# Attention blocks of six matmul rounds against a round of maxima and blocks of five

## The chip, the cores and the metric

The kernel runs on one core of one Trainium2 chip. The metric is the device time of one execution in microseconds (us). A core has five engines that run side by side and wait for one another by semaphores: TensorE (PE in the profile; its weight loads are listed apart as PEld), VectorE (DVE), ScalarE (ACT), GpSimd (POOL) and SyncE (SP), which here only issues DMAs. TensorE writes into PSUM, which has eight banks of 512 fp32 columns; ScalarE and VectorE read them.

## The reference

The program is one network of three layers on x of 8 images x 128 channels x 1024 positions. The first, where the change lies, is attention with 8 heads of 16 channels over the 1024 tokens of an image:

```python
qkv = (tokens @ w_proj + b_proj).reshape(B, N, NUM_HEADS, 3 * HEAD_DIM)
q, k, v = jnp.split(qkv, 3, axis=-1)
attn = jnp.einsum('bihd,bjhd->bijh', q, k) * SCALE
attn = jax.nn.softmax(attn, axis=2)
res = jnp.einsum('bijh,bjhd->bihd', attn, v).reshape(B, N, NUM_HEADS * HEAD_DIM)
out = res @ w_out + b_out + tokens
```

A spiking attention and a mixture of experts with 8 experts follow on its result; the change does not touch them.

## The kernel before

**Steps and blocks.** The attention goes through 16 steps (8 images, two groups of four heads each), and each step through 16 blocks, so 256 blocks. A block holds four score tiles, one for each head: 128 keys x 512 queries in one PSUM bank. A score tile is the sum of two matmuls on different halves of TensorE's rows: its A half contracts rows 0 to 49, its B half rows 64 to 111 (three bf16 parts stand for one fp32 number, and the two extra rows of the A half carry the subtracted maximum). An A matmul and a B matmul that stand side by side run at the same time; such a pair is called a round. ScalarE then takes exp of each tile (L644) into the tile `probs`, and four fp32 matmuls that run beside one another multiply it with v (L556, called pv). The pv of block t-1 is issued behind the rounds of block t.

**Maxima.** Softmax needs the row maximum of scores before exp. So the same scores are also computed the other way round, 128 queries x 512 keys, as two half tiles for each of 512 "maxima": one on A rows (L507, from `twin_q` and `twin_k`), one on B rows (L505, from the stacks). VectorE reduces each half tile to its maximum (L730) in the order in which they were filled; 1024 reductions in all. They run ahead of the scores that need them: the first 22 maxima are made before the first block, and a job called "solo" is one round that holds both halves of one maximum. A normal block makes two maxima, four half tiles; the last 13 blocks have none left to make.

**Banks.** Score tiles and the results of most side jobs share a ring of four PSUM banks (`ring`), taken in turn in the order in which they are begun; a bank can be begun again when ScalarE has read it. Half tiles of maxima and the transposes of the attention's result ("oturn") share a second ring of three banks (`slot`), which VectorE reads. `acc`, where pv sums up, is the eighth bank. TensorE works strictly in order: an instruction whose bank is not free holds up everything behind it.

**Order.** `job_order` gives each job a number, sorts by it, and all engines run through this one list. Between the pv of block t-1 and block t+1 there may be side jobs: "proj" and "v" (projections of the next image), "mturn" (a small matmul, L582, that turns 16 finished maxima into rows; result in the ring, taken by ScalarE at L677), "oturn" (L607; result in the slots, taken by VectorE at L769 and L771), "back", "out" and "bias" (results in the ring, taken by ScalarE), and, on VectorE alone, the statistics of finished tokens (L781, L787). Of the 243 blocks with maxima to make, 92 have nothing on TensorE between the pv before them and themselves, and do not follow an oturn with statistics; these are called plain blocks below. 29 have an mturn there, 29 an oturn, and 7 come straight behind an oturn block and statistics. The other 86 have a proj, v, back, out or bias there. The last 13 blocks, without maxima, are 8 plain ones, one with an mturn, two with an oturn, one with a back and one with an out.

**Rounds.** `ROUNDS` says what stands in a block's rounds. In a pair the first number is what goes on the A rows, the second on the B rows; 0 to 3 are the block's score tiles, 4 and 5 its first and second maximum. The first time that a number appears the tile is begun, the second time a score tile is finished. ScalarE's exps stand in the order in which tiles are finished, the ring banks in the order in which they are begun.

Of the kernel before, what the change touches and what calls it, by code (L numbers as in the profile page):

```python
# [45 lines left out]
BLOCKS = 2 * KT  # L46
# [9 lines left out]

ROUNDS = ((0, 4), (1, 5), (2, 0), (3, 1), (4, 2), (5, 3))


def side_jobs(s):

    b, g = s // G, s % G
    jobs = [(10 if g == 0 else 26 - BLOCKS, "oturn", (s, 0))]
    if s:
        jobs.append((2, "oturn", (s - 1, 1)))
    for n in (0, 1):
        q = 2 * s + 1 + n
        if q < 2 * UNITS:  # L70
            jobs.append((5 if q == 1 else 4 + 8 * n, "mturn", (q,)))
    if g == 0:
        if b + 1 < B:
            jobs += [(at, "proj", (b + 1, n)) for n, at in enumerate((0, 1, 3, 5))]
        if b:
            jobs += [(6, "back", (b - 1, 1)), (8, "out", (b - 1, 2)), (9, "out", (b - 1, 3))]
        else:
            jobs.append((7, "bias", ()))
    else:
        if b + 1 < B:  # L80
            jobs += [(6, "v", (b + 1, 0)), (8, "v", (b + 1, 1))]
        jobs += [(13, "back", (b, 0)), (14, "out", (b, 0)), (15, "out", (b, 1))]
    return jobs


def job_order():

    placed = []

    def put(at, kind, args):  # L90
        placed.append((at, len(placed), kind, args))

    m = AHEAD_FIRST
    for t in range(STEPS * BLOCKS):
        maxima = min(2, 2 * UNITS * QB - m)
        put(10 * t, "block", (t // BLOCKS, t % BLOCKS, m, maxima))
        put(10 * t + 12, "pv", (t // BLOCKS, t % BLOCKS))
        m += maxima
        if t % 2 and m < 2 * t + 2 + AHEAD_MAX and maxima:
            for n in range(2):  # L100
                put(10 * t + 7, "solo", (m + n,))
            m += 2
    for s in range(STEPS):
        for at, kind, args in side_jobs(s):
            t = s * BLOCKS + at
            put(10 * t + 4, kind, args)
            if kind == "out":
                put(10 * t + 23, "stats", args)
                put(10 * t + 42, "aggr", args)
    t = 10 * STEPS * BLOCKS + 20  # L110
    for n, (kind, args) in enumerate([("oturn", (STEPS - 1, 1)), ("back", (B - 1, 1)),
                                      ("out", (B - 1, 2)), ("out", (B - 1, 3)), ("stats", (B - 1, 2)),
                                      ("stats", (B - 1, 3)), ("aggr", (B - 1, 2)), ("aggr", (B - 1, 3))]):
        put(t + n + 30, kind, args)
    placed.sort(key=lambda j: j[:2])
    first = [("proj", (0, n)) for n in range(4)] + [("v", (0, n)) for n in range(2)]
    first += [("solo", (n,)) for n in range(QB + 1)] + [("mturn", (0,))]
    first += [("solo", (n,)) for n in range(QB + 1, AHEAD_FIRST)]
    return first + [j[2:] for j in placed]


def halves(job):
# [8 lines left out]
    met, out = set(), []  # L131
    for pair in ROUNDS:
        for tile, n in enumerate(pair):
# [17 lines left out]


ORDER = job_order()
USES = [use for job in ORDER for use in begun_by(job)]
S_USE = {use: n for n, use in enumerate(u for u in USES if u[0] in S_KINDS)}
# [1533 lines left out]
```

## Time and profile before

| what | us |
| --- | --- |
| median of 3 runs | 1243.26 (1242.04 to 1245.73) |
| the profiled execution's own time | 1240.29 |
| its span (first to last instruction) | 1238.5 |
| TensorE busy | 1094.5 |
| VectorE busy | 877.3 |
| ScalarE busy | 806.8 |
| GpSimd busy | 307.6 |

The profile is one execution. A page gives sums by engine and by group of instructions; the timeline gives instructions in order of time. In the timeline neighbouring instructions of one line are merged into one row with a count, whose duration reaches from the first start to the last end; a bracket names the idle time of the engine before the row and what ended it. The attention takes the span from about 60 to 806 us; the granted clock of TensorE is at its full level there.

### The profile page before, as it was taken

Reading aid. Unit: us, or ns where it says so; the run is one execution under the profiler, and the core shown is the slowest. Engines: PE = TensorE matmul, PEld = TensorE weight load, DVE = VectorE, ACT = ScalarE, POOL = GpSimd, SP = SyncE. Lnnn points to the kernel's source line nnn. Section 1 sums busy time; section 2 is a strip of 40 time slices with the busy share of each in tenths; the row PEclk is TensorE's granted clock in tenths of the full one; section 3 lists DMA queues with packets and bytes.
Section 4 is the critical chain, followed back from the end, with each engine's and each line's share of the span. In section 5 each row is a group of like instructions: output and inputs, shape, how many; then the busy total and the mean of one; then the engine's idle time right before and its main releaser. Section 6 shows DMA issues by size and latency. Waiting matters only on the chain. (4 is left out here: it accounts for less than half of the span.)

```text
span 1238.5 us, 23604 instructions
## 1 busy us (share of the span) xinstructions
PE 1094.5 (88%) x8048; PEld 537.0 (43%) x8048; DVE 877.3 (71%) x1988; ACT 806.8 (65%) x1732; POOL 307.6 (25%) x375
## 2 busy tenths in 40 slices
PE   5999999999999999999999999988877653898974
PEld 2123333333333333333333333335645443888873
DVE  4899879879879878988988988516565633444435
ACT  2177777777777777777877877865756541455542
POOL 4131041041041032022113100104354333444440
PEclk7699999999999999999999999998889855999996
DMA  5528028018108206405504600006000001222219
GB/s 128 106 70 158 1 60 150 27 34 171 25 2 179 48 1 143 85 2 105 123 2 92 120 2 2 18 1 169 19 26 27 24 28 54 62 62 61 62 46 272
DMA packets 73355, 85.52 MB, mean 69 GB/s; under 512 B 15656, under 2 KB 57256, under 8 KB 71704
## 3 DMA queue, kind: packets, MB, share of 16 engines
q1 hardware_dynamic: 64248, 72.65, 27.1%
q0 software_dynamic: 4320, 8.89, 2.0%
q10 hardware_dynamic: 4672, 2.49, 0.9%
q8 instruction: 68, 1.11, 0.4%
q14 instruction: 47, 0.39, 0.1%
HBM read 57.08 MB, written 26.65 MB: 68 GB/s over the span
## 5 line engine op out<-in xcount | busy, mean ns | idle before, releaser
L730 DVE TENSOR_REDUCE neg_half<-slot 128x1 f32<-128x512 f32 x1024 | 633.8, 682 | 101.5 <-PE slot L505 84.1
L644 ACT ACTIVATE probs<-ring 128x512 f32<-128x512 f32 x1024 | 528.7, 603 | 135.1 <-PE ring L514 132.6
L514 PE MATMUL ring<-stack_q,stack_k 50*128 50x512 bf16 (+1 forms) x2048 | 419.2, 382 | 2.0
L556 PE MATMUL acc<-probs,v_sb 128*32 128x512 f32 x2048 | 272.7, 605 | 0.1
L514 PEld LDWEIGHTS ring<-stack_q,stack_k 50*128 50x128 bf16 (+1 forms) x2048 | 151.9, 93 | 257.1 <-issue 109.3
L507 PE MATMUL slot<-twin_k,twin_q 48*128 48x512 bf16 x512 | 182.7, 391 | 20.4 <-DMA twin_q<-parts_dram 12.3
L505 PE MATMUL slot<-stack_k,stack_q 48*128 48x512 bf16 x512 | 162.1, 392 | 2.8 <-DVE neg_half L730 2.8
L1502 ACT ACTIVATE hid_t<-ps_h,b_of 128x128 f32<-128x128 f32 x284 | 80.9, 368 | 79.5 <-PE ps_h L1466 74.6
L424 POOL CAST m_parts<-neg_max 128x16 bf16<-128x16 f32 x32 | 6.3, 196 | 380.2 <-DVE neg_max L736 380.2
L1446 POOL DMA_INDIRECT rows_tok<-y,x_in x71 | 71.1, 1001 | 99.2 <-DVE y L1526 99.2
L1466 PE MATMUL ps_h<-xt,w_of 128*128 128x128 f32 x568 | 78.2, 282 | 17.6 <-DVE w_of L1516 16.6
L507 PEld LDWEIGHTS slot<-twin_k,twin_q 48*128 48x128 bf16 x512 | 47.5, 93 | 95.1 <-DVE neg_half L730 73.0
L993 POOL DMA_INDIRECT rows_in<-z_all,pos x64 | 62.7, 980 | 100.8 <-DVE pos L1325 76.5
L1466 PEld LDWEIGHTS ps_h<-xt,w_of 128*128 128x128 f32 x568 | 70.6, 196 | 21.0 <-DVE w_of L1516 19.4
L1475 PE MATMUL ps_y<-w_sb,hid_t 128*128 x568 | 75.8, 277 | 0.4 <-ACT hid_t L1502 0.4
L1475 PEld LDWEIGHTS ps_y<-w_sb,hid_t 128*128 128x128 f32 x568 | 69.8, 194 | 0.6 <-issue 0.6
L556 PEld LDWEIGHTS acc<-probs,v_sb 128*32 128x32 f32 x2048 | 40.3, 108 | 58.0 <-issue 52.0
L1164 ACT ACTIVATE mask<-bank 128x512 bf16<-128x512 f32 (+1 forms) x80 | 33.5, 465 | 45.4 <-PE bank L1075 43.3
L440 POOL CAST parts<-full 128x512 bf16<-128x512 f32 x28 | 17.1, 610 | 149.6 <-ACT full L687 149.6
L1526 DVE TENSOR_TENSOR y<-ps_y,b_sb 128x128 f32<-128x128 f32 x71 | 20.5, 289 | 40.1 <-PE ps_y L1475 38.6
L471 POOL TENSOR_SCALAR xr<-xr,b_sum 128x1024 f32<-128x1024 f32 x8 | 22.8, 2844 | 94.2 <-DMA xr<-in_x 94.2
L1515 DVE COPY b_of<-b_sb 128x4 f32 x71 | 11.9, 167 | 39.9 <-issue 22.2
(161 smaller groups left out, 1146.3 us busy)
## 6 DMA issues: line engine op xcount, KB each, us to landing
parts_dram<-parts SPq DMA_DIRECT2D x30, 384.0 KB, 5.7
stack_k<-parts_dram SPq DMA_DIRECT2D x16, 384.0 KB, 6.2
stack_q<-parts_dram SPq DMA_DIRECT2D x32, 192.0 KB, 7.5
x_in<-rows_in SPq DMA_DIRECT2D x71, 64.5 KB, 1.9
xp<-in_x SPq DMA_DIRECT2D x8, 512.0 KB, 4.6
stack_k<-parts_dram SPq DMA_DIRECT2D x16, 256.0 KB, 3.8
xr<-in_x SPq DMA_DIRECT2D x8, 512.0 KB, 4.5
out<-out_t SPq DMA_DIRECT2D x16, 256.0 KB, 2.1
```

Source lines behind the costliest of these rows:

```text
L505: return pe.matmul(out[:, :], stack_q[u % STACK_BUFS][rows, qhalf, h, cols], stack_k[u % STACK_BUFS][rows, h, HALF:N], start=True, stop=True)
L507: return pe.matmul(out[:, :], twin_q[u % TWIN_BUFS][:, qhalf, h, cols], twin_k[u % TWIN_BUFS][:, h, :], start=True, stop=True)
L514: return pe.matmul(out[:, :], stack_k[s % STACK_BUFS][rows, h, kt * P:(kt + 1) * P], stack_q[s % STACK_BUFS][rows, half, h, :], start=star ...
L556: mm = pe.matmul(acc[32 * h:32 * h + 32, :], v_sb[s // G % 2][:, kt, s % G * HG + h, :], probs[:, j % PROBS, h, :], start=(kt == 0), stop= ...
L644: act.activation(probs[:, j % PROBS, h, :], ring[n % S_BANKS][:, :], ACT.Exp).then_inc(s_empty[n % S_BANKS], 1)
L730: dve.tensor_reduce(neg_half[q % 2][:, half, k:k + 1], slot[n % M_BANKS][:, :], AX.X, ALU.max, negate=True).then_inc(m_empty[n % M_BANKS], 1)
L993: pool.indirect_dma_start(rows_in, bass.IndirectOffsetOnAxis(ap=pos[:, t:t + 1], axis=0), z_all[:, t, :], None).then_inc(s_sent, 16)
L1164: act.activation(mask[b % 2][:, m, lo:hi], bank_of(job)[:, 0:hi - lo], ACT.Sign).then_inc(s_taken["act"], 1)
L1446: pool.indirect_dma_start(rows_tok, bass.IndirectOffsetOnAxis(ap=x_in[:, s % X_RING, C:C + 1].bitcast(U32), axis=0), y[:, s % Y_RING, :], ...
L1466: mm = pe.matmul(ps_h[s % 2][:, k * P:(k + 1) * P], w1_of[:, s % 2, k * P:(k + 1) * P], xt[:, s % 2, :], start=True, stop=True)
L1475: mm = pe.matmul(ps_y[s % 2][:, 0:C], hid_t[:, s % 2, k * P:(k + 1) * P], w2_flat[:, bass.ds(start + k * C, C)], start=(k == 0), stop=(k = ...
L1502: last = act.activation(hid_t[:, s % 2, k * P:(k + 1) * P], ps_h[s % 2][:, k * P:(k + 1) * P], ACT.Gelu, bias=b1_of[:, s % 2, k:k + 1])
```

## The change

A block has five rounds in place of six and only one of its two maxima in them. The other maximum becomes a solo round, which the list places directly in front of the block, behind the pv and the side jobs that precede it. The rounds are numbered r1 to r6 before; after it the solo round is called r0 and the block's rounds r1 to r5. The four half tiles of maxima are called x0 to x3 and the score tiles s0 to s3. Tile s2 is now begun on the B rows and finished on the A rows. The last 13 blocks, which make no maxima, have no solo round.

```diff
--- before.py
+++ after.py
@@ -56,7 +56,7 @@
 
 
 
-ROUNDS = ((0, 4), (1, 5), (2, 0), (3, 1), (4, 2), (5, 3))
+ROUNDS = ((0, 4), (1, 2), (3, 0), (2, 1), (4, 3))
 
 
 def side_jobs(s):
@@ -93,7 +93,9 @@
     m = AHEAD_FIRST
     for t in range(STEPS * BLOCKS):
         maxima = min(2, 2 * UNITS * QB - m)
-        put(10 * t, "block", (t // BLOCKS, t % BLOCKS, m, maxima))
+        if maxima:
+            put(10 * t - 1, "solo", (m,))
+        put(10 * t, "block", (t // BLOCKS, t % BLOCKS, m + 1, maxima // 2))
         put(10 * t + 12, "pv", (t // BLOCKS, t % BLOCKS))
         m += maxima
         if t % 2 and m < 2 * t + 2 + AHEAD_MAX and maxima:
```

**TensorE, a plain block (step 7), before.** L514 with a `ring` bank is a half of a score tile, L505 and L507 with a `slot` bank a half tile of a maximum; two rows make a round.

```order
L514 MATMUL ring2<-stack_q2,stack_k2 128x512
L505 MATMUL slot2<-stack_k0,stack_q0 128x512
L514 MATMUL ring3<-stack_q2,stack_k2 128x512
L505 MATMUL slot0<-stack_k0,stack_q0 128x512
L514 MATMUL ring0<-stack_q2,stack_k2 128x512
L514 MATMUL ring2<-stack_q2,stack_k2 128x512
L514 MATMUL ring1<-stack_q2,stack_k2 128x512
L514 MATMUL ring3<-stack_q2,stack_k2 128x512
L507 MATMUL slot1<-twin_k0,twin_q0 128x512
L514 MATMUL ring0<-stack_q2,stack_k2 128x512
L507 MATMUL slot2<-twin_k0,twin_q0 128x512
L514 MATMUL ring1<-stack_q2,stack_k2 128x512
```

**The same place after.** All line numbers of the changed kernel are higher by two here.

```order
L509 MATMUL slot2<-twin_k0,twin_q0 128x512
L507 MATMUL slot0<-stack_k0,stack_q0 128x512
L516 MATMUL ring2<-stack_q2,stack_k2 128x512
L507 MATMUL slot1<-stack_k0,stack_q0 128x512
L516 MATMUL ring3<-stack_q2,stack_k2 128x512
L516 MATMUL ring0<-stack_q2,stack_k2 128x512
L516 MATMUL ring1<-stack_q2,stack_k2 128x512
L516 MATMUL ring2<-stack_q2,stack_k2 128x512
L516 MATMUL ring0<-stack_q2,stack_k2 128x512
L516 MATMUL ring3<-stack_q2,stack_k2 128x512
L509 MATMUL slot2<-twin_k0,twin_q0 128x512
L516 MATMUL ring1<-stack_q2,stack_k2 128x512
```

The half tiles of maxima stood in rounds 1, 2, 5 and 6; now two stand in r0, one in r1 and one in r5. The score tiles are begun in rounds 1, 2, 2 and 3 of the block in place of 1, 2, 3 and 4, counted from the first round behind the pv in rounds 2, 3, 3 and 4.

**TensorE around an oturn (step 7), before.** The transpose takes slot0.

```order
L556 MATMUL acc<-probs,v_sb0 32x512 x4
L607 MATMUL slot0<-ident,o_sb 128x128 x4
L514 MATMUL ring2<-stack_q2,stack_k2 128x512
L505 MATMUL slot1<-stack_k0,stack_q0 128x512
L514 MATMUL ring3<-stack_q2,stack_k2 128x512
L505 MATMUL slot2<-stack_k0,stack_q0 128x512
L514 MATMUL ring0<-stack_q2,stack_k2 128x512
L514 MATMUL ring2<-stack_q2,stack_k2 128x512
L514 MATMUL ring1<-stack_q2,stack_k2 128x512
L514 MATMUL ring3<-stack_q2,stack_k2 128x512
L507 MATMUL slot0<-twin_k0,twin_q0 128x512
```

**The same place after.**

```order
L558 MATMUL acc<-probs,v_sb0 32x512 x4
L609 MATMUL slot0<-ident,o_sb 128x128 x4
L509 MATMUL slot1<-twin_k0,twin_q0 128x512
L507 MATMUL slot2<-stack_k0,stack_q0 128x512
L516 MATMUL ring2<-stack_q2,stack_k2 128x512
L507 MATMUL slot0<-stack_k0,stack_q0 128x512
```

Slot0, which the oturn has filled, was asked for again in the block's fifth round (the last row before, x2); it is now asked for in r1, the sixth row after, also by x2.

**ScalarE, the exps of a block and the m_rows of an mturn behind them, before and after.** The number behind `ring` is the bank.

```order
L644 ACTIVATE probs<-ring0 128x512
L644 ACTIVATE probs<-ring1 128x512
L644 ACTIVATE probs<-ring2 128x512
L644 ACTIVATE probs<-ring3 128x512
L677 ACTIVATE m_rows1<-ring0 32x128
L644 ACTIVATE probs<-ring1 128x512
```

```order
L646 ACTIVATE probs<-ring0 128x512
L646 ACTIVATE probs<-ring2 128x512
L646 ACTIVATE probs<-ring1 128x512
L646 ACTIVATE probs<-ring3 128x512
L679 ACTIVATE m_rows1<-ring0 32x128
L646 ACTIVATE probs<-ring1 128x512
```

The second and the third exp have changed places; nothing else has moved on ScalarE, and on VectorE, GpSimd and SyncE nothing at all.

## Rows read from the trace of the kernel before

**Rows 1.** The page: span, then each engine's busy time, share and instructions.
```profile
span 1238.5 us, 23604 instructions
...
PE 1094.5 (88%) x8048; PEld 537.0 (43%) x8048; DVE 877.3 (71%) x1988; ACT 806.8 (65%) x1732; POOL 307.6 (25%) x375
```

**Rows 2.** The page's costliest groups: out<-in, count | busy us, mean ns | idle before, releaser.
```profile
L730 DVE TENSOR_REDUCE neg_half<-slot 128x1 f32<-128x512 f32 x1024 | 633.8, 682 | 101.5 <-PE slot L505 84.1
```

**Rows 3.** Waits of TensorE's weight loads, 100 to 780 us: total us, times, longest.
```profile
PEld slot L507 <- DVE neg_half L730: 58.7, 224, 0.5
```

**Rows 4.** Timeline, 316 to 327 us: start, duration, engine, line, tiles, count [idle before].
```profile
318.44 5.06 DVE L730 TENSOR_REDUCE neg_half<-slot 128x1 f32<-128x512 f32 x8 [1.13 <-PE slot L505]
...
320.56 0.09 PEld L514 LDWEIGHTS ring<-stack_q,stack_k 50*128 50x128 bf16 x1 [0.84 <-issue]
...
321.00 0.61 PE L514 MATMUL ring<-stack_q,stack_k 50*128 50x512 bf16 x4
...
321.44 0.38 PE L507 MATMUL slot<-twin_k,twin_q 48*128 48x512 bf16 x1
...
321.51 2.06 ACT L644 ACTIVATE probs<-ring 128x512 f32<-128x512 f32 x4 [0.51 <-PE ring L514]
...
321.76 0.09 PEld L507 LDWEIGHTS slot<-twin_k,twin_q 48*128 48x128 bf16 x1 [0.23 <-DVE neg_half L730]
...
322.09 0.16 PEld L556 LDWEIGHTS acc<-probs,v_sb 128*32 128x32 f32 x8 [0.23 <-issue]
...
323.08 0.97 PEld L598 LDWEIGHTS ring<-w_all,xp 128*128 128x128 f32 x8 [0.84 <-issue]
```

**Rows 5.** Timeline of VectorE, 300 to 400 us: four reductions that are ready in time.
```profile
346.09 2.48 DVE L730 TENSOR_REDUCE neg_half<-slot 128x1 f32<-128x512 f32 x4 [1.13 <-PE slot L505]
```

**Rows 6.** Timeline, 329 to 332 us: a block with an output transpose (L607) before it.
```profile
329.27 0.42 PEld L607 LDWEIGHTS slot<-ident,o_sb 128*128 128x128 f32 x4 [0.84 <-issue]
...
329.86 0.09 PEld L514 LDWEIGHTS ring<-stack_q,stack_k 50*128 50x128 bf16 x1 [0.17 <-issue]
...
330.26 0.42 DVE L771 TENSOR_TENSOR o_t<-slot,inv 128x256 f32<-128x256 f32 x1
...
330.61 7.55 DVE L730 TENSOR_REDUCE neg_half<-slot 128x1 f32<-128x512 f32 x12
...
330.74 0.09 PEld L507 LDWEIGHTS slot<-twin_k,twin_q 48*128 48x128 bf16 x1
...
331.66 0.16 PEld L556 LDWEIGHTS acc<-probs,v_sb 128*32 128x32 f32 x8 [0.23 <-ACT probs L644]
```

**Rows 7.** Timeline, 333 to 337 us: a block with a turn of the maxima (L582) before it.
```profile
333.61 2.06 ACT L644 ACTIVATE probs<-ring 128x512 f32<-128x512 f32 x4 [0.73 <-PE ring L514]
...
334.18 0.16 PEld L556 LDWEIGHTS acc<-probs,v_sb 128*32 128x32 f32 x8 [0.23 <-issue]
...
335.21 0.09 PEld L514 LDWEIGHTS ring<-stack_q,stack_k 50*128 50x128 bf16 x1 [0.48 <-ACT probs L644]
...
335.72 0.24 PEld L514 LDWEIGHTS ring<-stack_q,stack_k 50*128 50x128 bf16 x4 [0.40 <-ACT probs L644]
...
336.74 0.16 PEld L556 LDWEIGHTS acc<-probs,v_sb 128*32 128x32 f32 x8 [0.23 <-issue]
```

**Rows 8.** Timeline of TensorE, 382 to 388 us: the block behind an output transpose with statistics.
```profile
382.52 0.39 PE L505 MATMUL slot<-stack_k,stack_q 48*128 48x512 bf16 x1
...
384.66 1.07 PE L556 MATMUL acc<-probs,v_sb 128*32 128x512 f32 x8
...
385.66 0.39 PE L505 MATMUL slot<-stack_k,stack_q 48*128 48x512 bf16 x1
...
387.43 1.06 PE L556 MATMUL acc<-probs,v_sb 128*32 128x512 f32 x8
```

**Rows 9.** Timeline, 793 to 796 us: blocks at the end, without maxima.
```profile
793.64 1.20 PEld L514 LDWEIGHTS ring<-stack_q,stack_k 50*128 50x128 bf16 x8 [0.84 <-ACT probs L644]
...
795.07 0.16 PEld L556 LDWEIGHTS acc<-probs,v_sb 128*32 128x32 f32 x8 [0.23 <-issue]
```

## The prediction

> **What bounds the kernel now.** I read the page first. TensorE is busy for 1094.5 of 1238.5 us [rows 1], which names it as the engine to look at but does not say that it is the bound: a stalled matmul pair hardly shows as idle. VectorE's reductions of the maxima are next, 633.8 us [rows 2]. Then the waits: TensorE's loads for L507 waited for VectorE's reductions 224 times, 58.7 us in all [rows 3], about once in each block that makes maxima. So the question is what closes the loop from block to block, and that only the timeline tells.
>
> A plain block [rows 4]: r1 starts at 320.56, r3 at 321.00, r5 at 321.44, so rounds that wait for nothing are 0.22 apart. r6 starts at 321.76, released by VectorE, 0.10 later than 0.22 would have it. pv starts at 322.09, 0.33 later, and what stands behind it starts at 323.08, 0.99 later. Rounds 1.53 + pv 0.99 = 2.52 us for a block.
>
> Why r6 waits: its half tile x3 takes the bank of x0, three slots before. Four reductions that are ready in time take 2.48, each one 0.68 long and the next started 0.60 later (0.68 + 3 x 0.60) [rows 5]. Eight over two plain blocks took 5.06 [rows 4], so the fifth began 5.06 - 2.48 = 2.58 after the first, at 321.02: 0.46 after its round r1. The bank was free again 0.74 later, at 321.76. The loop that sets a plain block is therefore r1, +0.46 reduction of x0, +0.74 r6, +0.33 pv, +0.99 next r1 = 2.52. VectorE works 4 x 0.60 = 2.40 of these and TensorE without the wait would need 2.42: both are near the bound, neither is it alone.
>
> ScalarE: its exps start 0.51 after r3 (321.00 to 321.51) and four take 2.06 [rows 4]; TensorE goes on 0.05 after the last one ends (333.61 + 2.06 = 335.67, load at 335.72) [rows 7]. So the bank of s3 is free 0.51 + 2.06 + 0.05 = 2.62 after r3.
>
> **The change part by part.** No matmul, reduction or exp is added or taken away. In 243 blocks six rounds stay six (r0 to r5); in the last 13 one round goes. What changes is when banks are asked for.
>
> *The present loop* is still there: x0 is now in r0, its bank is wanted in r5 (x3). r0 +0.46 +0.74 = 1.20, +0.33 +0.99 = 2.52. No block gets shorter by it.
>
> *Maxima, new loop.* x2 of the next block stands in r1 and wants the bank of x3. x3 is the fourth reduction and starts at 0.46 + 3 x 0.60 = 2.26 after r0; its bank is free at 3.00. The next r0 is at 2.52 and its r1 would be at 2.74, so r1 waits 0.26; r5, 0.88 behind it, then comes 0.16 later than 1.20. The block after has slack again. So lengths go 2.52, 2.68, mean 2.60: +0.08.
>
> *Exps, new loop.* s3 is begun in r3, the same round in which s0 is finished. From r3 to the next r3 it takes at least 2.62. Before, s3 was begun in r4, so this loop asked for 2.62 - 0.22 = 2.40 and was hidden by 2.52. It is now the longest: a plain block takes 2.62, **+0.10**, and the loop of the maxima (2.60) lies inside it. 92 plain blocks x 0.10 = 9.2 us.
>
> *Blocks with an mturn.* The mturn takes the ring bank of s0, so that s2 wants the one of s3. It costs TensorE almost nothing: from pv at 334.18 to r1 at 335.21 is 1.03 [rows 7]. Before, s2 came in the third round, waited 0.07 (335.72 in place of 335.65) and pv followed 1.53 after r1 (336.74), as in a plain block. Now s2 is begun in r2, the round ahead of r3. r3 to pv is 0.44 + 0.33 = 0.77, to the next r0 +1.03 = 1.80; the bank is free at 2.62, so r2 stands at 0.82 after r0, and three rounds (0.66) and 0.33 later is pv: 1.81 against 1.53. **+0.28** x 29 = 8.1 us.
>
> *Blocks with an oturn.* The oturn takes a slot bank and VectorE frees it late: r1 of the block starts at 329.86, VectorE's L771 ends at 330.26 + 0.42 = 330.68, and the round that wants the bank starts at 330.74 [rows 6]. That was the fifth round, 0.88 after r1, where it would have stood anyway. Now it is r1: it waits until 0.88 after r0 instead of 0.22, r5 comes at 1.76, pv at 2.09; before pv was at 1.80 (331.66). **+0.29** x 29 = 8.4 us. In 7 of these VectorE also has statistics to do, and the block behind took 1.77 from r1 to pv (385.66 to 387.43) because VectorE was behind [rows 8]. With the later start it has caught up and the block takes 0.86 + 0.77 = 1.63 by the loop of the exps: 7 x -0.14 = -1.0 us.
>
> *Blocks with other side jobs*, 86: they hold TensorE long enough for ScalarE to finish. The bank that comes late there is the side job's own; s3 wants it, in the fourth round behind the job before and after. At nothing; if ScalarE were late by 0.05 each, 4 us.
>
> *The end.* Without maxima a block took 1.43 (793.64 to 795.07) [rows 9] + 0.99 = 2.42. One round less would make 2.20, but the loop of the exps has no maxima in it and holds here too: 2.62. 8 plain blocks x +0.20 = 1.6; the mturn block about +0.2; the two with an oturn, which waits for nothing here, 2 x -0.22: together +1.4. In this stretch several matmuls in a row stand on the same rows of TensorE, and the six rounds still took 5 x 0.22 + 0.33 = 1.43 [rows 9], so no weight load shows.
>
> The Trainium skill (TensorE: Matmul & The Clock Gate, "The mechanism") says that weights are loaded beside running matmuls when they go to other rows or into the background buffer, and its list of what overlaps that this needs different row groups. By the latter the old order would have shown a load in four places of these rounds and the new one in two, and the end would win more. The trace disagrees, as no load shows in the 1.43.
>
> **Sum.** 9.2 + 8.1 + 8.4 - 1.0 + 0 + 1.4 = +26.1 us on the profiled execution's 1240.3: 1266.4. That execution is 3.0 below the median shown, 1243.3; I forecast the median, **1269**.
>
> **The rivals.**
> 1. *The loop of the exps does not bind*, because ScalarE frees banks in another rhythm than I take from merged rows. Then the maxima alone cost: 92 x 0.08 = 7.4, oturn 7.4, mturn 29 x 0.08 = 2.3, and the end wins 13 x 0.22 = 2.9: +14.2, 1257. For it: exps have 0.5 of idle time in each block [rows 4]. Against: rows 7 show TensorE waiting for just this bank.
> 2. *VectorE is the bound* and moving banks about changes nothing: 8 reductions in 5.06 look like 0.63 each, and 4 x 0.63 = 2.52. Only the end wins, -2.9: 1240, within 0.3%. Against: four reductions also take 2.48 [rows 5], so 0.60 is its pace.
> 3. *Faster.* Two half tiles handed over at once fill VectorE's queue, and the wait of r6 vanishes: 243 x 0.11 = 26.7, with the end 29.6: 1214. It decides at whether x0's bank is free when r5 comes: free at 1.20, r5 at 1.10 after r0. A bank free 0.10 earlier would do it, but reductions last 0.68 each time.
> 4. *The loops add up* where I take the longer: plain blocks +0.18 instead of +0.10, 7.4 more, and a few tenths behind each output transpose: some +10, 1279.
>
> **How the numbers follow.** Forecast 0.66, rival 1 0.14, rival 2 0.05, rival 3 0.03, rival 4 0.12. The range runs from just below rival 1 to rival 4: 1256 to 1281. A difference of 0.3% (3.7 us) is about what a measurement of this kernel tells from none. Faster 0.03, same 0.05, slower 0.92.
>
> **What the profile after would show.** r0 to r0 of 2.62 in plain blocks, with TensorE held at the loads of r3 by L646 (the exps); VectorE's four reductions again 0.60 apart with a gap of 0.2; in mturn blocks a wait of 0.4 at r2 for L646; in oturn blocks one of 0.6 at r1 for VectorE's second operation on the transpose; VectorE and ScalarE as busy in us as before. Waits of L509 for reductions fall in number, those of the ring for ScalarE rise from few to over a hundred. It would be wrong if plain blocks stay at 2.52, or if they go to 2.42 with r5 unhindered.

## The result, and the profile after

The changed kernel takes 1272.75 us (median of 4 runs, 1271.13 to 1275.34), the kernel before 1244.39 (4 runs, 1242.04 to 1245.73). The ratio is 1.022, 95% interval 1.0193 to 1.0246: 28.4 us slower. The forecast was 1269, range 1256 to 1281, and slower. Of the runs of the kernel before that stand beside the experiments below, one took 1398.31 us at a mean granted clock of 0.725, and the ratios leave it out.

The profiled execution after has a span of 1269.3 us and a time of its own of 1271.13; its span is 30.8 us longer than the one of before [rows 1]. The page, as in rows 1 and 2: busy us (share of the span) and count of each engine, then the two groups that fill VectorE and ScalarE, with busy us, mean ns of one, and idle time before them.

```profile
span 1269.3 us, 23596 instructions
...
PE 1117.8 (88%) x8040; PEld 522.3 (41%) x8048; DVE 879.9 (69%) x1988; ACT 804.1 (63%) x1732; POOL 307.2 (24%) x375
...
L732 DVE TENSOR_REDUCE neg_half<-slot 128x1 f32<-128x512 f32 x1024 | 634.8, 683 | 125.9 <-PE slot L509 121.8
...
L646 ACT ACTIVATE probs<-ring 128x512 f32<-128x512 f32 x1024 | 528.6, 603 | 196.1 <-PE ring L516 195.3
```

VectorE's reductions are where they were: 634.8 us against 633.8 [rows 2]. What grew is TensorE's busy time, from 1094.5 [rows 1] to 1117.8, with the same matmuls. A matmul lasts 0.38 and the next one starts 0.22 after it where nothing waits [rows 4], so the first 0.16 of a wait shows as busy and not as idle. So the page tells that nothing was added and not where the time went. The waits of TensorE's weight loads do, here of the changed kernel, 100 to 800 us (who waits <- for whom: us in all, times, longest), against rows 3:

```profile
PEld ring L516 <- ACT probs L646: 52.0, 146, 0.4
PEld slot L509 <- DVE neg_half L732: 43.3, 142, 0.8
PEld slot L507 <- DVE o_t L773: 24.4, 28, 1.1
...
PEld slot L507 <- DVE neg_half L732: 12.7, 50, 0.4
```

and of the kernel before, 100 to 780 us:

```profile
PEld ring L514 <- ACT probs L644: 23.2, 50, 0.8
...
PEld slot L507 <- DVE o_t L771: 3.3, 7, 0.5
```

Three waits have moved. The score ring now waits for the exps 146 times instead of 50. The wait for VectorE's second operation on the output transpose, o_t, comes 28 times instead of 7. The wait for reductions, 224 times at L507 before, is spread over two lines, the A halves (L509, in r0 and r5) and the B half of r1 (L507). Of the 142 waits of L509, 30 are the 0.84 that follows every pv, some 25 of the 43.3 us, and cost nothing.

**A plain block after**, timeline of the changed kernel (start, duration, engine, line, tiles, count [idle before]), against rows 4:

```profile
332.65 2.06 ACT L646 ACTIVATE probs<-ring 128x512 f32<-128x512 f32 x4 [0.57 <-PE ring L516]
332.90 0.16 PEld L558 LDWEIGHTS acc<-probs,v_sb 128*32 128x32 f32 x8 [0.23 <-issue]
333.89 0.09 PEld L509 LDWEIGHTS slot<-twin_k,twin_q 48*128 48x128 bf16 x1 [0.84 <-DVE neg_half L732]
...
334.28 0.09 PEld L507 LDWEIGHTS slot<-stack_k,stack_q 48*128 48x128 bf16 x1 [0.28 <-DVE neg_half L732]
...
334.77 0.27 PEld L516 LDWEIGHTS ring<-stack_q,stack_k 50*128 50x128 bf16 x4 [0.38 <-ACT probs L646]
...
335.29 2.06 ACT L646 ACTIVATE probs<-ring 128x512 f32<-128x512 f32 x4 [0.57 <-PE ring L516]
335.54 0.16 PEld L558 LDWEIGHTS acc<-probs,v_sb 128*32 128x32 f32 x8 [0.23 <-issue]
```

The four exps end at 332.65 + 2.06 = 334.71, and r3 starts at 334.77, 0.06 behind them. The next exps start 0.52 later, pv 0.77 later. From pv to pv it is 335.54 - 332.90 = 2.64, and the exps' starts are 2.64 apart too, 335.29 - 332.65, with 0.57 of idle ScalarE between them. r1 waits as well, 0.39 behind r0 in place of 0.22, but r3 would wait until 334.77 whatever r1 did. VectorE of the changed kernel in such a stretch:

```profile
313.59 2.48 DVE L732 TENSOR_REDUCE neg_half<-slot 128x1 f32<-128x512 f32 x4 [0.15 <-PE slot L509]
316.23 2.48 DVE L732 TENSOR_REDUCE neg_half<-slot 128x1 f32<-128x512 f32 x4 [0.15 <-PE slot L509]
```

Four reductions still take 2.48, as in rows 5, now with a gap of 0.15 in each block.

**A block with an mturn**, against rows 7:

```profile
323.53 2.06 ACT L646 ACTIVATE probs<-ring 128x512 f32<-128x512 f32 x4 [0.57 <-PE ring L516]
323.77 0.16 PEld L558 LDWEIGHTS acc<-probs,v_sb 128*32 128x32 f32 x8 [0.23 <-issue]
...
324.80 0.09 PEld L509 LDWEIGHTS slot<-twin_k,twin_q 48*128 48x128 bf16 x1 [0.47 <-issue]
...
325.64 0.21 PEld L516 LDWEIGHTS ring<-stack_q,stack_k 48*128 48x128 bf16 x3 [0.38 <-ACT probs L646]
...
326.63 0.16 PEld L558 LDWEIGHTS acc<-probs,v_sb 128*32 128x32 f32 x8 [0.33 <-issue]
```

r2, which begins s2, stands 0.84 after r0 (324.80 to 325.64) and 0.05 behind the last exp, 323.53 + 2.06 = 325.59. pv comes 1.83 after r0; the forecast had 0.82 and 1.81.

**A block with an oturn**, against rows 6:

```profile
342.84 0.42 PEld L609 LDWEIGHTS slot<-ident,o_sb 128*128 128x128 f32 x4 [0.84 <-issue]
...
343.43 0.09 PEld L509 LDWEIGHTS slot<-twin_k,twin_q 48*128 48x128 bf16 x1 [0.17 <-issue]
...
343.83 0.42 DVE L773 TENSOR_TENSOR o_t<-slot,inv 128x256 f32<-128x256 f32 x1
...
344.30 0.09 PEld L507 LDWEIGHTS slot<-stack_k,stack_q 48*128 48x128 bf16 x1 [0.77 <-DVE o_t L773]
...
345.50 0.16 PEld L558 LDWEIGHTS acc<-probs,v_sb 128*32 128x32 f32 x8 [0.41 <-issue]
```

L773 ends at 344.25, and r1 starts 0.05 later, 0.87 after r0. pv is 2.07 after r0 against 1.80 before.

**The last blocks**, without maxima, loads of TensorE, against rows 9:

```profile
836.66 0.11 PEld L516 LDWEIGHTS ring<-stack_q,stack_k 50*128 50x128 bf16 x4 [0.40 <-ACT probs L646]
...
837.42 0.16 PEld L558 LDWEIGHTS acc<-probs,v_sb 128*32 128x32 f32 x8 [0.23 <-issue]
...
840.06 0.16 PEld L558 LDWEIGHTS acc<-probs,v_sb 128*32 128x32 f32 x8 [0.23 <-issue]
```

The same 2.64 with a round less: r3 waits for the exps, where before the blocks of six rounds, 2.42 long, waited for nothing.

**All blocks.** Mean us from one pv to the next, worked out from the starts of the pv rows in the two timelines; step 0 stands apart, since its first blocks wait for inputs.

| block | count | before | after | sum of the difference |
|---|---|---|---|---|
| plain | 84 | 2.533 | 2.638 | +8.8 |
| mturn | 28 | 2.560 | 2.858 | +8.3 |
| oturn | 21 | 3.403 | 3.687 | +6.0 |
| oturn with statistics | 7 | 3.727 | 4.007 | +2.0 |
| the one behind those | 7 | 2.773 | 2.600 | -1.2 |
| other side jobs | 80 | | | -0.9 |
| last, plain | 8 | 2.420 | 2.624 | +1.6 |
| last, others | 5 | 3.062 | 3.014 | -0.2 |
| step 0 | 14 | 3.191 | 3.557 | +5.1 |

With +0.8 before the first pv (57.17 to 58.01) this gives, up to rounding, the +30.4 from span start to the last pv (826.41 to 856.78).

Step 0 is the one place where the two profiled executions differ for another reason as well. Windows of both, with length, busy us (count) of PE, PEld, DVE, ACT and POOL, and then the granted TensorE clock. Before:

```profile
70.00:80.00 10.00, 9.65 (x70) 2.96 (x70) 8.64 (x16) 7.14 (x15) 7.63 (x10) 1.00 0.01 3
```

After:

```profile
70.00:80.00 10.00, 9.32 (x43) 2.48 (x44) 6.92 (x12) 4.03 (x9) 6.02 (x7) 0.66 0.01 2
```

A mean of 0.66 is a stretch at 1.2 GHz for about two thirds of these 10 us and at 2.4 for the rest; 43 matmuls were done in place of 70. Blocks 4 and 5 of step 0 took 6.01 and 2.52 before, and 7.33 and 4.37 after, 3.2 in all; less the 0.1 that the change costs a plain block anyway, about 3 of the 30.8 is this fall of the clock. Block 7 took 2.97 in place of 2.52, and this is not the clock: with the solo round behind the block, where the clock is at 1.00 all through, it also took 2.97. The clock fell in variants of the kernel before too, as the last section lists.

### The profile page after: what moved, and what is told of

Its sections match the earlier page's. It is cut to its first block and busy times, and to the rows that moved or that the text cites. A ratio compares the mean times of both kernels' runs of the same rounds, so it can differ in the third digit from the quotient of the medians.

```text
span 1269.3 us, 23596 instructions
## 1 busy us (share of the span) xinstructions
PE 1117.8 (88%) x8040; PEld 522.3 (41%) x8048; DVE 879.9 (69%) x1988; ACT 804.1 (63%) x1732; POOL 307.2 (24%) x375
## 5 line engine op out<-in xcount | busy, mean ns | idle before, releaser
L732 DVE TENSOR_REDUCE neg_half<-slot 128x1 f32<-128x512 f32 x1024 | 634.8, 683 | 125.9 <-PE slot L509 121.8
L516 PE MATMUL ring<-stack_q,stack_k 50*128 50x512 bf16 (+1 forms) x2048 | 382.0, 384 | 5.0 <-ACT probs L646 0.3
L509 PE MATMUL slot<-twin_k,twin_q 48*128 48x512 bf16 x512 | 201.4, 395 | 12.8 <-DMA twin_q<-parts_dram 12.3
L507 PE MATMUL slot<-stack_k,stack_q 48*128 48x512 bf16 x512 | 179.9, 397 | 13.6 <-DVE o_t L773 10.9
L516 PEld LDWEIGHTS ring<-stack_q,stack_k 50*128 50x128 bf16 (+1 forms) x2048 | 120.4, 94 | 165.3 <-ACT probs L646 70.9
L509 PEld LDWEIGHTS slot<-twin_k,twin_q 48*128 48x128 bf16 x512 | 47.7, 94 | 178.6 <-issue 99.6
L507 PEld LDWEIGHTS slot<-stack_k,stack_q 48*128 48x128 bf16 x512 | 41.3, 93 | 58.2 <-DVE neg_half L732 30.0
```

The lines of the kernel that those rows point to most:

```text
L507: return pe.matmul(out[:, :], stack_q[u % STACK_BUFS][rows, qhalf, h, cols], stack_k[u % STACK_BUFS][rows, h, HALF:N], start=True, stop=True)
L509: return pe.matmul(out[:, :], twin_q[u % TWIN_BUFS][:, qhalf, h, cols], twin_k[u % TWIN_BUFS][:, h, :], start=True, stop=True)
L516: return pe.matmul(out[:, :], stack_k[s % STACK_BUFS][rows, h, kt * P:(kt + 1) * P], stack_q[s % STACK_BUFS][rows, half, h, :], start=star ...
L732: dve.tensor_reduce(neg_half[q % 2][:, half, k:k + 1], slot[n % M_BANKS][:, :], AX.X, ALU.max, negate=True).then_inc(m_empty[n % M_BANKS], 1)
```

## The experiments

All ratios are against runs of the kernel before that were taken beside the experiment on the same chip. Their medians are 1244.01 us (solo round behind, short reductions, transpose inside in the kernel before), 1241.88 (short exps, transpose inside in the changed kernel, old table at the end) and 1242.75 (both halved). The changed kernel itself stands beside 1244.39 alone, so a difference in us between it and an experiment is uncertain by some 2.5. Two kernels with the same edit were taken side by side, except for those with the transpose inside. Block times are means of the same kind as in the table, from one profiled execution of each kernel. How far they repeat is seen from the kernel with the old table in its last blocks, which until there is the changed kernel: its plain, mturn and oturn blocks have the same means within 0.002.

### Where the solo round stands: behind the block

The new table of five rounds is kept; the solo round moves from in front of the block to behind its last round, ahead of pv.

```diff
-            put(10 * t - 1, "solo", (m,))
-        put(10 * t, "block", (t // BLOCKS, t % BLOCKS, m + 1, maxima // 2))
+        put(10 * t, "block", (t // BLOCKS, t % BLOCKS, m, maxima // 2))
+        if maxima:
+            put(10 * t + 1, "solo", (m + 1,))
```

> The five-round table stays, but the solo round stands behind the block's five rounds, ahead of pv, in place of in front of them. Theory A (two loops: the ring of score tiles through ScalarE costs plain blocks 0.10 and mturn blocks 0.28; the slots through VectorE cost the oturn blocks 0.29): the half tile that wants the oturn's slot comes last in the block again, so oturn blocks go back from 3.69 to 3.40 from pv to pv. Plain blocks stay at 2.62 to 2.64 and mturn blocks at 2.84, since s3 and s2 are begun in the same rounds. The round of s3 is now 0.22 nearer to the side job in front, so proj, v and back blocks, which wait for ScalarE to take the side job's result, go up by 0.22 (proj 3.72 to 3.94). In all about +31 us on the kernel before, 1275. Theory B (the slots alone make the difference; the table of five rounds is harmless): plain and mturn blocks fall back to 2.52 and 2.56, and the whole to within 5 us of the kernel before. Theory C (the solo round itself costs, two half tiles at once): all blocks as in the changed kernel, oturn blocks too, about 1273.

Measured: 1280.18 us (1278.13 to 1281.43), ratio 1.0283, interval 1.0256 to 1.031. Slower than the changed kernel, as the loop of the exps wants: behind the block the solo round no longer separates s3 from the next block's start, so blocks whose side job had hidden the loop pay 0.2 more (v 3.657 to 3.874, back 3.195 to 3.394, proj 3.724 to 3.941), and plain blocks stay long, at 2.675 (2.638 in the changed kernel).

It is 5 us over what was expected. oturn blocks took 3.65, where 3.40 was expected (28 x 0.25 = 7.0), and plain blocks 0.04 more than 2.64; mturn blocks took 2.73 and not 2.84, which gives 3 us back and was not followed up. Timeline of this kernel, 317 to 319 us:

```profile
317.19 0.42 PEld L609 LDWEIGHTS slot<-ident,o_sb 128*128 128x128 f32 x4 [0.84 <-issue]
...
318.10 0.26 DVE L771 RECIPROCAL inv<-slot 128x16 f32<-128x16 f32 x1
318.39 0.42 DVE L773 TENSOR_TENSOR o_t<-slot,inv 128x256 f32<-128x256 f32 x1
```

x3 is now asked for in the last round, so VectorE is still at it when the transpose arrives: its first operation starts 0.91 after the transpose, and the second ends at 318.81. In the kernel before the second ended 1.41 after the transpose [rows 6], here 1.62. I had left the reductions that stand ahead of it out of account. What waits is x3: it takes the bank of x0, whose reduction stands behind these two operations, and its load starts at 319.47.

### Reductions at half the width, in both kernels

```diff
-                dve.tensor_reduce(neg_half[...], slot[n % M_BANKS][:, :], AX.X, ALU.max,
+                dve.tensor_reduce(neg_half[...], slot[n % M_BANKS][:, 0:HALF // 2], AX.X, ALU.max,
```

> The kernel before, with each reduction of a maximum reading 256 of its 512 columns (half of the keys are left out of the maximum). A reduction should then last about 0.41 in place of 0.68 (estimate: 0.68 less 256 columns at the pace that 0.68 for 512 bounds). Theory A: x0's bank is free before r6, plain blocks go from 2.52 to 2.42 where TensorE itself and the loop of the exps (2.40) stand; oturn blocks from 3.40 to about 3.0; mturn blocks stay at 2.56 to 2.62; proj, v, back stay. About -24 us in the blocks, and up to 12 more in the solo rounds at the start, which run at VectorE's pace: 1208 to 1221.

> The changed kernel with the same halved reductions. Theory A: plain blocks stay at 2.62, mturn blocks at 2.84 to 2.86, oturn blocks at 3.67, since ScalarE and the oturn's own operations set them: only 2 us less in the blocks, and the same up to 12 at the start: 1259 to 1271, and 45 to 50 us slower than the kernel before with halved reductions (the gap of 28 nearly doubles). Theory B (VectorE's slots make the difference): with reductions of 0.41 no slot is late, and the gap to the kernel before with halved reductions shrinks to under 5 us.

Measured: before with short reductions 1213.54 us (1211.98 to 1214.33), ratio 0.9741, interval 0.9715 to 0.9766. After with short reductions 1264.12 (1259.71 to 1265.38), ratio 1.0145, interval 1.0111 to 1.0179. The same edit wins some 30 us in the kernel before and 9 in the changed one; the gap between them grows from 28 to 50.6. The page of the kernel before with this edit shows that the reductions really are short:

```profile
L730 DVE TENSOR_REDUCE neg_half<-slot 128x1 f32<-128x256 f32 x1024 | 384.2, 420 | 303.0 <-PE slot L505 254.5
```

The changed kernel with it, waits of TensorE's loads, 100 to 800 us:

```profile
PEld ring L516 <- ACT probs L646: 76.0, 234, 0.6
...
PEld slot L507 <- DVE o_t L773: 22.4, 28, 0.8
```

No row for a reduction is left, and the exps are waited for 234 times. A plain block of it, timeline:

```profile
319.85 2.06 ACT L646 ACTIVATE probs<-ring 128x512 f32<-128x512 f32 x4 [0.63 <-PE ring L516]
...
321.96 0.17 PEld L516 LDWEIGHTS ring<-stack_q,stack_k 50*128 50x128 bf16 x4 [0.39 <-ACT probs L646]
...
322.49 2.06 ACT L646 ACTIVATE probs<-ring 128x512 f32<-128x512 f32 x4 [0.57 <-PE ring L516]
```

The last exp of the block before had ended at 321.91 (319.85 + 2.06); r3 starts 0.05 later. Plain blocks take 2.633, against 2.638 with full reductions: 250 us less of VectorE's work move them by 0.005. Before, they fall from 2.533 to 2.436. So VectorE's reductions bound the plain block of the kernel before by a bank, the changed kernel's plain block does not hang on them, and a rival in which the reductions are behind its loss is refuted. The oturn blocks tell a second thing: 3.135 before, 3.681 after. With short reductions the whole price of the early r1 shows, 0.55; in the unedited kernels half of it (0.28) was paid already, as a wait for reductions that stood there before.

### Exps at half the width, in both kernels

The exps read 256 of 512 columns from the fifth block on, so that no part of probs is read before it is written.

```diff
-                act.activation(probs[:, j % PROBS, h, :], ring[n % S_BANKS][:, :],
+                w = HALF if s == 0 and j < PROBS else HALF // 2
+                act.activation(probs[:, j % PROBS, h, 0:w], ring[n % S_BANKS][:, 0:w],
```

> The kernel before, with each exp from the fifth block on working on 256 of its 512 columns (the other half of `probs` keeps old values). An exp should last about 0.38, as ScalarE's copy of 256 columns does, so four are done some 1.2 us after the first starts in place of 2.06. By theory A the loop of the exps is hidden in this kernel (2.40 against 2.52), so plain blocks stay at 2.52, mturn blocks at 2.54 to 2.56, oturn blocks at 3.40, and the whole at 1240 to 1244. If ScalarE were the bound it would fall by tens of us.

> The changed kernel with the same halved exps. Theory A: the loop of the exps is gone, what is left is the loop of the maxima. Plain blocks go from 2.64 to 2.60, mturn blocks from 2.86 to about 2.62, oturn blocks stay at 3.69, and the last 13 blocks go from 2.62 to 2.20. In all 14 us above the kernel before with halved exps, 1255, half of the loss. Theory B (slots alone): plain and mturn blocks do not move, 1270. Theory C (ring alone): plain, mturn and oturn blocks all as in the kernel before, 1240.

Measured: before 1243.74 us (10 runs, 1242.15 to 1245.24), ratio 1.0011, interval 0.9997 to 1.0025: nothing, so ScalarE did not bind the kernel before. After 1251.24 (1250.62 to 1252.83), ratio 1.009, interval 1.0072 to 1.0109: 21 us less than the changed kernel. The gap to the kernel before with the same edit is 7.5 in place of 28.4. So about three quarters of the loss go with the exps' length. Waits of the changed kernel with this edit, 100 to 800 us:

```profile
PEld slot L509 <- DVE neg_half L733: 49.0, 140, 0.8
PEld ring L516 <- PE ring L516: 45.2, 176, 0.3
PEld slot L507 <- DVE neg_half L733: 26.4, 96, 0.4
PEld slot L507 <- DVE o_t L774: 24.4, 28, 1.1
```

No row is left in which the loads of the score tiles (L516) wait for exps. The second row is TensorE waiting for its own earlier matmul; with both halved, below, it can be read alone. Of the gap of 7.5 us, where I expected 14, there is left by blocks: plain 2.560 against 2.530 (+0.03), mturn 2.640 against 2.560 (+0.08), oturn 3.686 against 3.402 (+0.28, untouched), last plain blocks 2.230 against 2.407 (-0.18). All but the first are near what was expected; the loop of the maxima was to give 2.60. Where plain blocks follow one another they take 2.52 and 2.64 by turns, the pattern of the forecast (2.52 and 2.68) with a smaller swing. Timeline of this kernel, where that loop alone is at work:

```profile
327.32 0.09 PEld L509 LDWEIGHTS slot<-twin_k,twin_q 48*128 48x128 bf16 x1 [0.84 <-DVE neg_half L733]
...
327.70 0.09 PEld L507 LDWEIGHTS slot<-stack_k,stack_q 48*128 48x128 bf16 x1 [0.28 <-DVE neg_half L733]
...
328.90 0.16 PEld L558 LDWEIGHTS acc<-probs,v_sb 128*32 128x32 f32 x8 [0.32 <-issue]
```

r1 is 0.38 behind r0, not the 0.48 of my sum, and pv 1.58 behind r0, only 0.05 more than the 1.53 of before [rows 4]: in this block the wait at r1 takes the place of the one at the last round instead of adding to it.

### Both halved

> The kernel before with reductions and exps both halved (256 of 512 columns). Theory A: both loops are gone and a block without side jobs stands at TensorE's own 2.42, one with an mturn at about 2.46 (2.59 with halved reductions alone, where the exps' loop held it), one with an oturn at 3.1. About 1211.

> The changed kernel with reductions and exps both halved. Theory A says that three separate mechanisms made the loss: the exps' loop, the maxima's loop, and the oturn's slot wanted in r1. Two are gone here, so plain blocks are at 2.42 and mturn blocks at 2.46 as in the kernel before with both halved; oturn blocks stay at 3.67 to 3.69 against 3.1, 29 x 0.5 = 15; the last 13 blocks win 2.9. So +12 us on the kernel before with both halved. If the table of five rounds or the solo round cost TensorE something of its own, plain blocks would differ too.

Measured: before 1206.92 us (1205.48 to 1207.85), ratio 0.9711, interval 0.9685 to 0.9737. After 1225.15 (1224.97 to 1227.31), ratio 0.9859, interval 0.9834 to 0.9883. With neither engine in the way the changed kernel is still 18.2 us behind. Oturn blocks account for 15.3 of it: 28 x (3.680 - 3.134). mturn blocks give 1.1, plain ones 84 x (2.450 - 2.419) = 2.6, and the last 8 plain blocks win 8 x (2.410 - 2.226) = 1.5. I had expected 12: 15 for the oturn blocks, which came true, and -2.9 for the end, which won only 2.0 in its 13 blocks; plain blocks, mturn blocks and those with other side jobs (1.1) were to cost nothing. The changed kernel with both edits, waits of TensorE's loads, 100 to 800 us:

```profile
PEld ring L516 <- PE ring L516: 33.9, 183, 0.3
...
PEld slot L507 <- DVE o_t L774: 22.4, 28, 0.8
```

The first row is TensorE waiting for its own earlier matmul in the ring, which with both edits in the kernel before comes once (0.3 us). The kernel lets the matmul that finishes a score tile wait until the one that began it has ended. Timeline of this kernel, the load that opens r4:

```profile
327.24 0.10 PEld L516 LDWEIGHTS ring<-stack_q,stack_k 50*128 50x128 bf16 x2 [0.16 <-PE ring L516]
```

It finishes s2, which r2 began at 326.77 with a matmul of 0.38, and stands 0.25 behind r3 (326.99) in place of 0.22. In r4 of the new table both halves finish a tile, the A half first; in the old one an A half only begins tiles or makes maxima. This fits the 0.03 that a plain block is longer, 84 x 0.03 = 2.5, but no run separates it. In the changed kernel without edits the same wait comes 86 times (20.9 us), and there r3's wait for the exps sets the plain block.

### The output transpose inside the block, in both kernels

If an oturn makes r1 wait because it takes a slot bank just ahead of it, then another place should cure that part alone. The block is cut in two jobs and the oturn stands between them: between r2 and r3 in the kernel before (CUT = 2), between the fourth and fifth round of the changed one (CUT = 4).

```diff
...
+        put(10 * t, "block", args)
+        if inside:
+            put(10 * t + 1, "rest", args)
...
-            put(10 * t + 4, kind, args)
+            put(10 * t + (10.5 if kind == "oturn" else 4), kind, args)
```

> The kernel before with its six-round table; only the 31 oturns that stood in front of a block stand inside it now, between r2 and r3. By theory A an oturn in front of a block delays the reduction of x0 by 0.29 (0.75 in place of 0.46 after r1), and r6 with it. Behind r2, VectorE has x0 and x1 to reduce while TensorE transposes, and r6, which comes 0.59 later by the oturn, finds x0's bank free: oturn blocks go from 3.40 to 3.12, and where statistics are done too from 3.73 + 2.78 to about 6.1 for the two blocks. 22 x 0.28 + 7 x 0.4 = 9 us less: about 1235. If the oturn costs what it costs by its length on TensorE alone, nothing changes: 1244.

> The changed kernel; the 31 oturns that stood in front of a solo round stand between r4 and r5 of the block now. Theory A: r1 no longer wants the oturn's slot, so VectorE's two operations on it are no longer in TensorE's way there. The oturn wants x0's bank and r5 x1's, both free about 0.2 later than 0.60 apart because VectorE joins the two halves' maxima in these blocks: oturn blocks go from 3.69 to about 3.32, the block behind goes up by 0.1 at most. About 8 to 10 us less than the changed kernel, 1262 to 1265. If the oturn cost in the changed kernel what it does by its length alone, nothing moves: 1272.

Measured, changed kernel: 1260.15 us (1257.47 to 1264.32), ratio 1.0151, interval 1.0133 to 1.0169, 12.6 less than the changed kernel (10 less, where each is set against its own runs of the kernel before: 18.3 above them in place of 28.4). oturn blocks 3.687 to 3.328 (3.32 expected). With the transpose inside, they are as long in both kernels (3.32 in the kernel before, below), so the 0.28 between them goes with its place.

Measured, kernel before: 1242.24 (10 runs, 1240.05 to 1246.83), ratio 0.9983, interval 0.9964 to 1.0002. Expected was 1235. oturn blocks went from 3.40 to 3.32, not to 3.12. Timeline of that kernel:

```profile
307.25 0.10 PEld L514 LDWEIGHTS slot<-stack_k,stack_q 48*128 48x128 bf16 x1
307.77 0.42 PEld L616 LDWEIGHTS slot<-ident,o_sb 128*128 128x128 f32 x4 [0.42 <-issue]
307.78 0.17 DVE L747 TENSOR_TENSOR neg_max<-neg_half 128x16 f32<-128x16 f32 x1
307.89 1.29 DVE L741 TENSOR_REDUCE neg_half<-slot 128x1 f32<-128x512 f32 x2
308.35 0.11 PEld L523 LDWEIGHTS ring<-stack_q,stack_k 50*128 50x128 bf16 x4 [0.17 <-issue]
...
309.23 0.09 PEld L516 LDWEIGHTS slot<-twin_k,twin_q 48*128 48x128 bf16 x1 [0.34 <-DVE neg_half L741]
```

The row of 307.25 is the weight load for r2, whose matmuls begin 0.22 behind r1's, at 307.46; the transpose follows 0.31 later, where a round would after 0.22. And another operation of VectorE (L747) stands ahead of x0's reduction, which begins 0.66 after its round's load (307.23) and not 0.46; so the last round still waits 0.34 for a bank. It is also another bank than I had expected: with the transpose's bank between x1 and x2, x3 takes the bank of x1 and no longer that of x0. The two reductions end at 307.89 + 1.29 = 309.18, and the round begins at 309.23. With the interval holding 1, this is no gain that could be claimed.

### The old table in the last blocks

```diff
+LAST_ROUNDS = ((0, 4), (1, 5), (2, 0), (3, 1), (4, 2), (5, 3))
...
-    for pair in ROUNDS:
+    for pair in ROUNDS if maxima else LAST_ROUNDS:
```

> The changed kernel with the table of six rounds in the last 13 blocks alone. Theory A: there the plain blocks go back from 2.62 to 2.42, the oturn blocks from 2.82 to 3.00, in all 1.4 us less; the blocks ahead are untouched. If fewer rounds were worth their 0.22 each and something else had eaten them, the plain blocks would be slower than 2.62.

Measured: one run, 1269.8 us; one run tells nothing of a difference this small. Its trace does: the last plain blocks take 2.421 in place of 2.624, at six rounds instead of five. A round more is 0.2 quicker, because s3 is begun a round later.

## Why the prediction was right

The time (1269 against 1272.75), the sign and the mechanisms held; the sum was 26.1, the blocks outside step 0 gave +24.4, and the sum had a part of step 0 in it, since it counts 92 plain blocks and the table 84. By its steps:

- *The loop of the exps is the bound of a plain block.* Predicted 2.62, measured 2.638, the 0.02 being that exps start 0.52 behind r3 and r3 0.06 behind their end. Shown from both sides: short reductions leave it where it was, short exps remove it. Rival 1 (it does not bind, 1257) and rival 2 (VectorE is the bound, 1240) fall by that.
- *The loop of the maxima, 2.60, lies inside it.* It does, but its size was wrong: alone it gives 2.56. It did not matter to the time, since the longer loop was right; of the 6.5 us by which I missed the run with short exps it explains 84 x 0.05, about 4.
- *mturn, +0.28 each.* Measured +0.30 (2.560 to 2.858). Most of it is the exps: with short ones +0.08 is left.
- *oturn, +0.29 each.* Measured +0.28, untouched by the exps' length. Halved reductions bring out 0.55: the forecast took its 1.80 of before from a block that already waited for VectorE, which was right for this kernel and would be half of the price in one with a faster VectorE. The 7 blocks behind: -0.17 each against -0.14.
- *Other side jobs at nothing.* Measured -0.9 over 80 blocks. The job covers the exps there; the solo round behind the block took that cover away, at 0.2 for each block.
- *The end, +1.4.* Measured +1.6 - 0.2 = +1.4. With both halved the round less was worth 0.18.
- *No weight load shows.* The list in the Trainium skill (TensorE: Matmul & The Clock Gate, "The mechanism"), by which only loads to different row groups overlap, would have let the end win more than a round's 0.22, as two pairs of neighbours on the same rows are left of four. The measured 0.18 with both halved is less than the round alone, so the trace does not bear this list out.
- *The loops do not add up* (rival 4, 1279): where r1 waits for a maximum, r3 waits that much less. Rival 3 (faster) would have needed r5 unhindered and nothing else late; the waits for the exps took its place.
- *What was to be seen in the profile*: waits of the ring for ScalarE "over a hundred" (146), waits of r2 of 0.4 (0.38), four reductions in 2.48 (yes) with a gap of 0.2 (0.15), r1 behind an oturn late by 0.6 (0.77 is the idle time before the load; 0.87 - 0.22 = 0.65 is the lateness), r0 to r0 of 2.62 in plain blocks (2.64), VectorE and ScalarE as busy as before (877.3 to 879.9 and 806.8 to 804.1).

What the sum did not have is most of step 0: +5.1, of which some 3 are the clock's fall in that one execution and 0.45 is block 7; the rest is plain, mturn and oturn blocks as elsewhere. The medians differ by 28.4 and hold whatever mix of clocks their runs had.

## What to carry to other kernels

Write down a loop for each ring of banks: from the request of a bank to its reader's last read, plus what TensorE does until it asks again. The longest is the block, and an order that shortens TensorE's part can lengthen another ring's; here a spare round between the request of a bank and the block's end was worth more than the round it cost. To find which engine binds, halve its work in both kernels: the answer is how the gap between them moves, not how busy the engine is. And a job that borrows a bank should stand where that bank is wanted last: with the transpose moved, the changed kernel won some 10 us. The kernel before won nothing that could be claimed; there the last round then wanted the bank of x1, which comes free later.

## What the runs showed of the hardware

- Pace and duration differ. A reduction of 128x512 is 0.68 us long and four take 2.48, so each starts 0.60 behind the last; one of 128x256 is 0.42 long. An exp of 128x512 is 0.60 long, and four take 2.06, 0.49 apart; of 128x256, 0.39 and four in 1.21, 0.27 apart.
- The granted clock of 60 to 80 us fell in some executions and not in others. In windows of 60 to 70 and 70 to 80 us it was, in the kernel before and its variants: 1.00 and 1.00 unedited, with short reductions and with both halved; 0.83 and 1.00 with short exps; 1.00 and 0.83 with the transpose inside. In the changed kernel and its variants: 1.00 and 0.66 unedited; 0.83 and 0.83 with the old table in the last blocks and with short exps; 0.74 and 0.83 with the transpose inside; 1.00 and 1.00 with the solo round behind, with short reductions and with both halved. From 80 to 100 us it was 1.00 in all twelve traces. The changed kernel and the one with the old table at its end run the same instructions until then, and still differ. Each kernel has one trace, so how often the clock falls in each is not known, and what sets it off I did not test. So two profiles can be 3 us apart in the start without the change having a part in it, and a comparison by block classes is safer than one by spans.
